# q and V of the local attention as three fp32r products of high and low halves, behind a later conv unit

## The reference

```
perceived = depthwise 3x3 conv of x, 3 outputs per channel, + b_perc
hid       = gelu(perceived @ w_up1 + b_up1)            # 384 -> 256, exact gelu
h         = x + hid @ w_up2 + b_up2                    # 256 -> 128
q, k, v   = h @ w_qkv.T + b_qkv
scores    = q . k over the 3x3 neighbours / sqrt(128)  # beyond the borders k and v are zero
out       = h + softmax(scores) @ v over the 3x3 neighbours
```

## Time and profile before

| what | value |
| --- | --- |
| median of three runs | 412.9 us (412.62 to 414.03) |
| the profiled execution | 412.48 us, span 410.7 us |
| granted clock, mean | 0.989 of full speed |
| busy: PE, DVE, ACT, POOL | 386.6, 317.5, 306.1, 183.3 us |
| share of PE in the chain that ended last | 78% (conv units 41%, scores 5%, V 7%, q 7%, up 9%, values 9%) |
| DMA | 28.57 MB, mean 70 GB/s |

### The profile page before, as it was taken

One profiled execution on the slowest core, in us unless ns is written; L12 is line 12 of the kernel. 1 busy time (PEld: TensorE's weight loads), 2 busy tenths in 40 slices (PEclk: granted clock), 3 DMA queues, 4 the chain that ended last, 5 costly groups with the idle time before them and its releaser, 6 DMA issues.

```text
span 410.7 us, 10251 instructions
## 1 busy us (share of the span) xinstructions
PE 386.6 (94%) x3618; PEld 353.2 (86%) x3618; DVE 317.5 (77%) x886; ACT 306.1 (75%) x681; POOL 183.3 (45%) x158
## 2 busy tenths in 40 slices
PE   2798898999999999999999999999999999999794
PEld 1698697898989999898989999898989989898484
DVE  4987868686878868686887868686897868784866
ACT  6533488877886987778786987778786987876782
POOL 6928663544434363544435364453435354230100
PEclk9979999999999999999999999999999999999998
DMA  8320020305031040404022040404022030301003
GB/s 251 139 65 1 19 100 0 117 2 168 2 116 52 18 152 0 166 0 165 1 85 81 9 157 0 166 0 165 1 70 96 0 102 2 104 15 40 0 25 131
DMA packets 11369, 28.57 MB, mean 70 GB/s; under 512 B 2385, under 2 KB 3025, under 8 KB 11345
## 3 DMA queue, kind: packets, MB, share of 16 engines
q1 hardware_dynamic: 10496, 28.20, 20.1%
q10 hardware_dynamic: 848, 0.05, 0.1%
HBM read 19.86 MB, written 8.39 MB: 69 GB/s over the span
## 4 chain that ended last, share of the span: by engine, by line
PE 78%; DVE 8%; ACT 3%; issue 2%; POOL 0%; DVEq 0%; ACTq 0%
PE m_ps L440 41%; PE s_ps L512 9%; PE work L450 9%; PE work L476 7%; PE work L471 7%; PE s_ps L495 5%; DVE t L799 2%; ACT p_sb L697 1%; DVE y L884 1%; DVE y L889 1%; DVE h_around L1016 1%; DVE ps_sb L873 1%; DVE y L887 1%; ACT m L619 1%; DVE ru_sb L874 0%
## 5 line engine op out<-in xcount | busy, mean ns | idle before, releaser
L440 PE MATMUL m_ps<-thi,whi 128*128 128x248 f32 (+1 forms) x576 | 171.1, 297 | 4.6 <-DVE wlo L812 2.7
L440 PE MATMUL m_ps<-thi,wlo 128*128 128x248 f32 (+1 forms) x576 | 161.7, 281 | 0.0
L440 PE MATMUL m_ps<-tlo,whi 128*128 128x248 f32 (+1 forms) x576 | 160.4, 278 | 0.0
L440 PEld LDWEIGHTS m_ps<-thi,whi 128*128 128x128 f32 x576 | 109.5, 190 | 11.6 <-issue 7.2
L440 PEld LDWEIGHTS m_ps<-tlo,whi 128*128 128x128 f32 x576 | 110.3, 191 | 4.2 <-issue 3.6
L440 PEld LDWEIGHTS m_ps<-thi,wlo 128*128 128x128 f32 x576 | 109.4, 190 | 0.0
L1106 POOL TENSOR_TENSOR hid_lo<-hid,hid_hi 128x1024 fp32r<-128x1024 f32 x30 | 71.9, 2396 | 20.8 <-ACT hid_hi L639 20.8
L683 ACT COPY pt<-ptc 32x256 f32<-32x256 f32 (+3 forms) x189 | 74.3, 393 | 5.8 <-DVE ptc L950 1.3
L629 ACT ACTIVATE hid<-y,b1eff 128x1024 f32<-128x1024 f32 x31 | 35.7, 1151 | 46.0 <-DVE y L897 25.5
L697 ACT ACTIVATE p_sb<-p_sb,negmax 128x101 f32<-128x101 f32 x128 | 47.0, 371 | 18.8 <-DVE negmax L931 18.8
L1113 POOL TENSOR_TENSOR p_sb<-p_sb,rsum 128x384 f32<-128x384 f32 x32 | 27.8, 870 | 68.0 <-DVE rsum L939 68.0
(11 more groups left out here) (124 smaller groups left out, 714.9 us busy)
## 6 DMA issues: line engine op xcount, KB each, us to landing
xp<-x_planes SPq DMA_DIRECT2D x16, 640.0 KB, 5.2
xr<-x_rows SPq DMA_DIRECT2D x16, 512.0 KB, 4.1
out<-o_sb SPq DMA_DIRECT2D x28, 256.0 KB, 4.1
out<-y SPq DMA_DIRECT2D x4, 256.0 KB, 2.1
w1T<-w SPq DMA_DIRECT2D x1, 384.0 KB, 3.1
w2T<-w SPq DMA_DIRECT2D x1, 128.0 KB, 4.3
wqk_in<-w_qk SPq DMA_DIRECT2D x1, 128.0 KB, 4.3
mask_bf<-masks SPq DMA_DIRECT2D x1, 126.2 KB, 4.2
```

The costliest lines, as they stand in the source:

```text
L440: last = pe.matmul(m_ps[:, b, col + first:col + end], a[:, j, dy, half * P:(half + 1) * P], c[:, par, T_PLACE[j], first + by:end + by], st ...
```

## The change

Two new tensors, h_hi and h_lo, hold the high and the low half of h. ACT writes h_hi (`high_h`, two halves of 512 columns), behind the high half of t of the next image and ahead of gelu of half 0. DVE writes h_lo (`low_h`), behind the third bank of half 0 and ahead of the low half of t. The weights of q and V get high and low halves too, in the set-up. q becomes two groups of three fp32r products of 512 columns, written to the s_ps banks in place of work banks. V becomes eight groups of three fp32r products with 130 columns (the zero key's column twice). On PE q and V stand together behind unit 8, the ninth of twelve, where before one part of V and q stood ahead of unit 8 and the rest of V behind it. Then comes unit 9, then the scores, then units 10 and 11; before, the scores stood ahead of units 9 to 11. The last attention keeps its fp32 products, with 130 columns for V.

```diff
-VT = C + 1
+VT = C + 2
...
+        h_hi = sb("h_hi", [P, PIX], F32R)
+        h_lo = sb("h_lo", [P, PIX], F32R)
+        wqk_hi = sb("wqk_hi", [P, C], F32R)
+        wqk_lo = sb("wqk_lo", [P, C], F32R)
+        wv_hi = sb("wv_hi", [P, VT], F32R)
+        wv_lo = sb("wv_lo", [P, VT], F32R)
...
+            def project_q_parts(n, c):
+                if from_image(n, 2):
+                    pe.wait_ge(rmax_done, n * 8 + (4 * c - 12))
+                if from_image(n, 3):
+                    pe.wait_ge(o_done, n * 2 + (c - 5))
+                cols = slice(c * CH, (c + 1) * CH)
+                pe.wait_ge(h_hi_done, n * 2 + (c - 1))
+                pe.matmul(s_ps[:, c, :], wqk_hi[:, :], h_hi[:, cols], start=True, stop=False)
+                pe.matmul(s_ps[:, c, :], wqk_lo[:, :], h_hi[:, cols], start=False, stop=False)
+                pe.wait_ge(h_lo_done, n * 2 + (c - 1))
+                pe.matmul(s_ps[:, c, :], wqk_hi[:, :], h_lo[:, cols], start=False, stop=True).then_inc(q_ready, 1)
+            def project_v_parts(n, part):
+                for u, i in enumerate(V_PARTS[part]):
+                    to, px = v_bank(n, part)[:, u * VT:(u + 1) * VT], slice(i * P, (i + 1) * P)
+                    pe.matmul(to, h_hi[:, px], wv_hi[:, :], start=True, stop=False)
+                    pe.matmul(to, h_hi[:, px], wv_lo[:, :], start=False, stop=False)
+                    last = pe.matmul(to, h_lo[:, px], wv_hi[:, :], start=False, stop=True)
+                last.then_inc(v_ready, 1)
...
-            def scores(n, hp):
-                for g in range(2):
-                    if from_image(n, 2):
-
-                        pe.wait_ge(rmax_done, n * 8 + (4 * g - 12))
-                    if from_image(n, 3) and not is_last(n):
-
-                        pe.wait_ge(o_done, n * 2 + (g - 5))
-                    score(n, hp, g)
...
+                    pe.wait_ge(wa_lo_done, 2)
...
-                units(6, 7)
-                if attn:
+                units(6, 7, 8)
+                if attn:
+                    for c in range(NCH):
+                        project_q_parts(n, c)
                     pe.wait_ge(h_done, n * 2)
-                    project_v(n, 1 - par, 0)
-                    project_q(n, 1 - par, 0, 2)
-                    project_q(n, 1 - par, 1, 0)
-                units(8)
-                if attn:
-
-                    pe.wait_ge(q_done, n * 2 - 1)
-                    project_v(n, 1 - par, 1)
-                    pe.wait_ge(q_done, n * 2)
-                    project_v(n, 1 - par, 2)
-                    scores(n, 1 - par)
-                units(9, 10, 11)
+                    for part in range(3):
+                        project_v_parts(n, part)
+                units(9)
+                if attn:
+                    for g in range(2):
+                        pe.wait_ge(q_done, n * 2 + (g - 1))
+                        score(n, 1 - par, g)
+                units(10, 11)
...
-            nc.scalar.mul(wvT[:, C:VT], wa[:, 2 * C:2 * C + 1], -SCALE).then_inc(wt_copied, 1)
+            nc.scalar.mul(wvT[:, C:VT], wa[:, 2 * C:2 * C + 1].to_broadcast([P, 2]), -SCALE).then_inc(wt_copied, 1)
+            nc.scalar.mul(wqk_hi[:, :], wa[:, C:2 * C], SCALE).then_inc(wa_hi_done, 1)
+            nc.scalar.copy(wv_hi[:, 0:C], wv_in[:, :]).then_inc(wa_hi_done, 1)
+            nc.scalar.mul(wv_hi[:, C:VT], wa[:, 2 * C:2 * C + 1].to_broadcast([P, 2]), -SCALE).then_inc(wa_hi_done, 1)
...
+            def high_h(n, hp, c):
+                act.wait_ge(h_done, n * 2 + (c - 1))
+                if from_image(n, 2):
+                    act.wait_ge(v_ready, n * 3 - 3)
+                nc.scalar.copy(h_hi[:, c * CH:(c + 1) * CH],
+                               h_of(n - 1, hp)[:, W + c * CH:W + (c + 1) * CH]).then_inc(h_hi_done, 1)
             def take_q(n, c):
                 act.wait_ge(q_ready, n * 2 + (c - 1))
-                nc.scalar.activation(q_sb[:, c * CH:(c + 1) * CH], work[:, 2 if c == 0 else 0, :],
+                sums = work[:, 2 if c == 0 else 0, :] if is_last(n) else s_ps[:, c, :]
+                nc.scalar.activation(q_sb[:, c * CH:(c + 1) * CH], sums,
                                      ACT.Identity, bias=bq_s[:, :]).then_inc(q_done, 1)
...
                 if more:
                     high_t(n + 1, 1 - par)
+                if attn:
+                    for c in range(NCH):
+                        high_h(n, 1 - par, c)
                 if conv:
                     gelu(n, 0)
...
+            def low_h(n, hp):
+                for c in range(NCH):
+                    cols = slice(c * CH, (c + 1) * CH)
+                    dve.wait_ge(h_hi_done, n * 2 + (c - 1))
+                    if from_image(n, 2):
+                        dve.wait_ge(v_ready, n * 3 - 3)
+                    nc.vector.tensor_tensor(h_lo[:, cols], h_of(n - 1, hp)[:, W + c * CH:W + (c + 1) * CH],
+                                            h_hi[:, cols].bitcast(F32), ALU.subtract).then_inc(h_lo_done, 1)
...
+            dve.wait_ge(wt_copied, 3)
+            dve.wait_ge(wa_hi_done, 3)
+            nc.vector.tensor_tensor(wqk_lo[:, :], wqk[:, :], wqk_hi[:, :].bitcast(F32), ALU.subtract).then_inc(wa_lo_done, 1)
+            nc.vector.tensor_tensor(wv_lo[:, :], wvT[:, :], wv_hi[:, :].bitcast(F32), ALU.subtract).then_inc(wa_lo_done, 1)
...
-                    z = v_bank(n, part)[:, 0:len(V_PARTS[part]) * VT].rearrange("p (t c) -> p t c", c=VT)[:, first:end, C:VT]
+                    z = v_bank(n, part)[:, 0:len(V_PARTS[part]) * VT].rearrange("p (t c) -> p t c", c=VT)[:, first:end, C:C + 1]
...
                 if conv:
                     finish_y(n, 0)
+                if attn:
+                    low_h(n, 1 - par)
                 if more and from_image(n, 2):
                     low_t(n + 1, 1 - par)
```

More of the change, by code:

```diff
@@ L257, in build @@
         hlo_done = sem("hlo_done")
+        h_hi_done = sem("h_hi_done")
+        h_lo_done = sem("h_lo_done")
         w2hi_done = sem("w2hi_done")
+        wa_hi_done = sem("wa_hi_done")
+        wa_lo_done = sem("wa_lo_done")
         w2lo_done = sem("w2lo_done")
```

## The result

The changed kernel takes 439.6 us (median of 4, 436.4 to 440.9) against 412.8 us: ratio 1.063, 95% interval 1.056 to 1.070. A second set of six executions, in the run called after_again, gave 439.3 us, 435.5 to 441.6. The forecast was 432, with 421 to 438 as its range: the direction was right, the size too small (19 us where 27 were measured). The profiled execution took 436.4 us (span 434.6), 23.9 more than that of before, where the sum had 19.3.

The account below looks back on a forecast made before the run. TensorE, busy throughout, was taken to bound the kernel, with a loop through ACT and DVE becoming longer: 2.4 + 14 x 24.4 - 324.7 = 19.3 us on the profiled 412.5 gives 431.8, said as 432 us; range 421 to 438.

Parts of the forecast that it names:

- the sum: Whole execution: 2.4 us in image 1 plus 16.9 us over 14 periods, 19.3 us slower.
- PE's work: TensorE per image: q 0.35 us less, V 0.89 us more, 23.22 to 23.76 us with nothing waiting.
- The floor under V's products: V's 24 products: the 128-column weight load, not columns, sets the pace, 111 ns each.
- rival (b): V: fp32r loads hidden, products at column pace, 58 to 65 ns; 413 to 415.5 us; chance 0.09.
- (c): V: fp32r products with few columns run slower, 217 ns at four clocks per column; 470 us; chance 0.04.
- The two loops: Per image: PE waits at unit 0 for m13's copy until S + 4.25, at q's third product until S + 19.80.
- rival (a): Steady images: ACT and DVE don't bind, both PE waits vanish, PE alone decides; 421 us; chance 0.13.
- S: Start of an image's scores; later moments are given as S plus so many us.
- the period is 24.4: Steady images: next scores come 24.4 us after the last, 0.65 more than PE's own work.
- the paragraph on PE alone: TensorE's work per image with nothing waiting: 23.76 us, a loss of 0.54 us in each of 15 images.
- Image 1: Scores of image 1 come later because the low halves of h are delayed: 2.4 us taken, from 1.1 to 2.6.
- The collision with POOL: Image 1: POOL's low half of t, 48.03 to 51.66 us, slows DVE's low_h; scores 2.6 us later if engines alternate.

Follow-up runs that it names:

- scores_early: Changed kernel with the scores moved back ahead of unit 9, so three units again follow them; 423.3 us, ratio 1.023.
- half_columns: Changed kernel with the second and third product of each V tile on 66 of 130 columns, weight loads as before; 439.2 us, ratio 1.060.
- high_h_first: Changed kernel with the high halves of h ahead of the high half of t in ACT's queue; 432.8 us, ratio 1.048.
- image1_native: Changed kernel with fp32 products straight from h in image 1 alone; 435.0 us, ratio 1.053.
- order_only: Changed kernel's new order without halves of h: q and V as fp32 products straight from h; 420.9 us, ratio 1.018.
- v_native: Changed kernel with V as eight fp32 products straight from h, q still in halves, same order; 423.1 us, ratio 1.024.

## Why the prediction was right about the direction and short of the size

**PE's work.** Right. q takes 1.39 us without a stop (1.37 forecast), V 2.63 (2.67 forecast), and scores_early runs at 23.76 us per image, which is the sum of the prediction to the digit. The floor under V's products holds for fp32r: half_columns shows it, and rival (b) falls. So does (c): 130 and 66 columns cost no more than the floor of 111 to 112 ns. The loads are as long with fp32 operands (V before) as with fp32r ones (V after):

```profile
L476 PEld LDWEIGHTS work<-wvT,h_around 128*128 128x128 f32 x240 | 29.2, 191 | 2.7 <-DVE h_around L1016 2.7
...
L505 PEld LDWEIGHTS work<-wv_hi,h_lo 128*128 128x128 f32 x120 | 23.1, 192 | 0.0
```

The Trainium skill ("TensorE: Matmul & The Clock Gate", weight-path modes) speeds up loads of 128 columns when the type is not FP32. With fp32r operands this case's traces do not bear a fast load out: the loads last 192 ns as above, and in half_columns a tile's three products take 0.33 us, 111 ns each.

**The two loops.** Right in their places and nearly right in their sizes, and rival (a) falls: with both waits gone the period is 23.8, with them 24.7. In the image whose timeline is shown S is 156.00. Unit 0 starts at S + 4.26, forecast S + 4.25, though the gap between the copy of m13 and unit 0, for which the prediction counted a load of 0.17 that no run shows by itself, is 0.14 in the chain. q's third product starts at S + 19.85, forecast S + 19.80. That the loops lie close together is shown by high_h_first, which gives 0.18 back of the 0.9; 0.15 was forecast for removing one wait alone. One reading was too generous and changed nothing: ACT is idle for 0.89 us ahead of its table load in that image of the kernel before, not for over 1 us.

**The step that failed** is a mis-sized term, "the period is 24.4": it measured 24.67, 0.27 more, and over 14 periods 3.8 us. Up to q's third product the path is right to 0.05 us. From there to the next scores the prediction has 4.63 us (0.23, 0.69, 2.67 and 1.04), and the timeline has 180.70 - 175.85 = 4.85. Two pieces are too small in it. The third product was priced as if nothing had stood still: 0.23, where 0.34 passes until the next start. And unit 9 was priced at 1.04, the pace in the middle of a stretch of units, where between V and the scores it takes 1.18. V is 0.04 shorter than forecast. The prediction's own numbers held a warning. Its path without the waits adds up to 1.46 + 2.08 + 14.94 + 0.46 + 4.63 = 23.57 us, while the paragraph on PE alone has 23.76 for the same work: the path has all twelve units at 1.04, 12.48 us, where the earlier trace rows has 7.49 + 2.08 + 2.08 + 1.03 = 12.68.

**Image 1** was forecast 2.4 us later and came 3.2 later (57.5 for 54.3), 0.8 us short. The collision with POOL is as described (high_h_first). From the start of h to the scores it takes 57.5 - 48.7 = 8.8 us, before 54.3 - 48.1 = 6.2. The difference is the 2.6 that the prediction worked out for engines that alternate, before it took 2.4. The other 0.6 is that h starts later, at 48.70 for 48.13. Whether this is the set-up's added operations, put at 0 to 0.4, or a difference between executions stays open: in the profiles of the versions, all with these operations, h starts between 47.75 and 48.70, and before has one profile. The two terms, 3.8 and 0.8, make the 4.6 us between 19.3 and the 23.9 measured on the profiled executions. The tail behind the scores of image 15 is 31.65 us in both profiles, as forecast.

**The median** is the other term that failed. The prediction took the distance from the profiled execution to the median from the kernel before, 0.4 us; after the change it is 3.2 us (439.6 and 436.4). Had the kernel kept to either of the forecast terms, its time would have been inside the range: 435.8 with the forecast period, 436.8 with the forecast distance. The prediction took no account of the clock. The kernel before has a stretch at half clock in the set-up, from 19.0 to 25.8 us. The profile of the changed kernel has one there too and a second from 42.1 to 45.6, which comes ahead of q in image 1 and so is not caused by the stops there (before the fall PE was busy for 1.18 us from 38.7 to 42.1). half_columns and scores_early have their second stretch behind the stops of image 1 instead, over V on the chain. In half_columns that makes 3.5 + 0.7 us of the 4.4 by which its profiled execution is longer than that of the changed kernel. image1_native brings the executions together and is 4.6 us shorter in the median, 0.8 in the profiled executions. That the longer executions of the changed kernel lose their time in just this way was not profiled. It is inferred from these runs and from the lower mean clock of the longer ones.

## What to carry to other kernels

Splitting an fp32 product into three fp32r products pays by columns and costs by loads: with 512 columns two instructions become three of half the length (1.72 to 1.39 us), with 130 columns each of the three costs the floor of 111 to 112 ns that goes with a load of 128 columns (1.78 to 2.63 us). A full TensorE says nothing on how much slack the loop through the other engines has: lay out the moments of one image from the scores to the next scores, and look where a moved step lets PE arrive ahead of the engine that frees its bank. Then take the waits out of that path again: what is left has to add up to the engine's own work per image, and here it was 0.19 us short. When a step is moved towards the end of an image, count the units that are left behind it, since they were the cover of somebody's copy.

## What the runs showed of the hardware beyond what was expected

- A stop of PE costs more than the idle time that the profile puts beside it: 0.45 us of idle time at unit 0 is a loss of 0.7 us, in order_only as in the changed kernel. By starts 0.6 of it is lateness and under 0.1 lies in the matmuls right behind.
- Products with a load of 128 weight columns follow each other at 111 to 112 ns, with 1 and 129 moving columns in fp32, with 130 in fp32r, and in half_columns, where two of three have 66, in the mean of a tile.
- DVE's subtraction with both inputs in SBUF took 2.69 us instead of 1.29 for two halves while POOL subtracted too, and 1.28 in the version in which POOL came later.
- TensorE's clock fell to 1.2 GHz in half_columns from 53.4 to 63.6 us; from 50.0 to the fall PE had been busy for 1.78 us. In the profile of the changed kernel it fell from 42.1 to 45.6 instead, and not behind the stops of image 1. Which of the two happens differs between profiles of kernels whose order of work is the same. In high_h_first, image1_native and v_native it also fell in the last image, and their tails took 32.9 us instead of 31.65.
